# Cross attention biases of Q, K and V added by ScalarE, and the causal diagonal masked by a minimum on VectorE behind the exponential

## The chip, the cores and the metric

The kernel runs on one core of a Trainium2 chip, in one launch. The metric is the device time in microseconds (us). The core has TensorE (PE) for matrix products, VectorE (DVE), ScalarE (ACT), GpSimd (POOL), and SyncE (SP), which here only issues DMAs. Each engine executes its own instructions in order; engines wait for each other by semaphores. Products accumulate in PSUM, in eight banks of 128 x 512 numbers; everything else lies in SBUF.

## What is computed

Eight sequences of 512 tokens with 512 features go through a gated cross attention and then a gated block of causal attention and a mixture of experts. Cut to what the change touches, with `y` the layer norm of `x` and `c` the context:

```python
# cross attention, 16 heads of 32
Q = (y @ Wq + bq).reshape(B, S, 16, 32)
K = (c @ Wk + bk).reshape(B, S, 16, 32)
V = (c @ Wv + bv).reshape(B, S, 16, 32)
scores = einsum('bqhd,bkhd->bhqk', Q, K) / sqrt(32) + rel_bias[:, rel_pos]
attn = softmax(where(key_padding_mask, -inf, scores))
x = x + tanh(g_xattn) * (einsum('bhqk,bkhd->bqhd', attn, V).reshape(B, S, D) @ Wo + bo)
...
# causal attention inside the second block, 16 heads
att = einsum('bhqd,bhkd->bhqk', q, k) / sqrt(64)
att = softmax(where(tril(ones((t, t))), att, -inf))
out = einsum('bhqk,bhkd->bhqd', att, v)
```

## The kernel before

The kernel runs three passes one after the other: pass A is the cross attention (about 0 to 923 us of the span), pass B the causal attention (to about 1848 us), pass C the experts. The change touches A and B, which are built alike.

Both work on one sequence (a batch) after another. A batch has 64 units: 16 heads in four groups of four (HG), times four blocks of 128 keys (NT), head fastest, so a group of heads is 16 steps. Everything is written as steps: each engine's function `body` counts 64 steps, and in each it issues its part, so the order of instructions on an engine is that of the program. In step s, TensorE computes the scores of unit s-6 transposed (keys in partitions, queries in columns; L747 in A, L1504 to L1506 in B) into one of two banks `st_bank`, and, for the unit s of the next group, the scores again with the queries in partitions (L760, L1521 and L1522), from which VectorE takes the row maximum (L615, L1384; semaphore `lowered`), which is later folded into the transposed scores as one more row of the contraction. ScalarE takes the exponential of the transposed scores into `pt` or `probs` (L497, L1258; semaphore `exped`). GpSimd adds the probabilities of the four key blocks for the softmax's sum (L404, L407, L1169; `pooled`). Every four steps TensorE multiplies four heads' probabilities with V (L774, L1535, "the AV products"; `summed`).

Between these, TensorE's `fill` issues pieces of jobs that a planner has given to steps: the projections Q, K, V and the output projection O, transposes, and the spreading of the softmax sums. A job's result lies in one of three banks until it is evicted. Numbers of high precision are carried as two float16 parts: a high half, written by ScalarE (L464 and L471 in A, L1224 in B), and a low half, written by VectorE as value minus high half (L579, L1335). A product then takes three matmuls per 128 of the contraction (L693; L1425 to L1427).

In pass A the biases are added by TensorE: at the end of each of the jobs Q, K, V and O, one matmul L695 over 512 columns multiplies the two float16 halves of the bias with a tile of ones. With 16 such jobs in a batch and 8 batches these are 128. The end of a group of heads is evicted on a fixed schedule: ScalarE copies the AV result to `o_un` (L523), VectorE transposes and inverts the sums (L564 to L568), GpSimd multiplies `o_un` with them (L425, `normed`), ScalarE writes the high half `o_hi` (L528) and GpSimd the low half (L428), which the O products need.

In pass B a causal diagonal block has to hide the keys behind the query. For the transposed scores TensorE adds, in the first 128 columns of each unit, the product of `far` (the identity times 1e15) and `hidden` (-1e30 times 1e-15 where the key is hidden, else 0), one matmul L1505 of 128 columns for each of the 512 units; the exponential of the result is zero. For the row maxima VectorE adds `tri`. Since the blocks lie in the lower triangle, a unit of key block j has 512 - 128 j columns of queries.

A bank of scores is used again by the unit after the next one, so L747 and L1504 wait for the exponential of the unit before the last.

## Time and profile before

| | |
|---|---|
| time, median of 3 runs | 2419.53 us (2417.91 to 2424.08) |
| the profiled execution, its own time | 2419.89 us |
| its span | 2418.0 us |
| TensorE busy | 2171.5 us (90%) |
| VectorE busy | 1514.7 us (63%) |
| GpSimd busy | 1365.2 us (56%) |
| ScalarE busy | 1197.2 us (50%) |
| TensorE clock granted, mean | 0.955 of full speed |

The profile is of one execution. The span lies within the program's time, which is 1.9 us longer. A busy share of the whole span is a mean over three passes with different limits, so the rows below are taken from stretches within a pass. In rows, tiles of pass A begin with `a_`, of pass B with `b_`, of pass C with `c_`. The duration of a matmul in a row is that of one that stands in a pipeline: the next one starts before it has ended, and what a matmul costs a busy TensorE is the distance between two starts.

### The profile page before, as it was taken

Reading aid. Unit: us, or ns where it says so; the run is one execution under the profiler, and the core shown is the slowest. Engines: PE = TensorE matmul, PEld = TensorE weight load, DVE = VectorE, ACT = ScalarE, POOL = GpSimd, SP = SyncE. Lnnn points to the kernel's source line nnn. Section 1 sums busy time; section 2 is a strip of 40 time slices with the busy share of each in tenths; the row PEclk is TensorE's granted clock in tenths of the full one; section 3 lists DMA queues with packets and bytes.
Section 4 is the critical chain, followed back from the end, with each engine's and each line's share of the span. In section 5 each row is a group of like instructions: output and inputs, shape, how many; then the busy total and the mean of one; then the engine's idle time right before and its main releaser. Section 6 shows DMA issues by size and latency. Waiting matters only on the chain. (4 is left out here: it accounts for less than half of the span.)

```text
span 2418.0 us, 50305 instructions
## 1 busy us (share of the span) xinstructions
PE 2171.5 (90%) x12864; PEld 982.9 (41%) x12865; DVE 1514.7 (63%) x4218; ACT 1197.2 (50%) x2316; POOL 1365.2 (56%) x1452
## 2 busy tenths in 40 slices
PE   3899999999999963899999999999985797899997
PEld 1333333333333311344444444444432343455554
DVE  3788888887888843556565565555533678344443
ACT  3355555554555442355545454454544574455554
POOL 3267677677677670264655564565561565455554
PEclk7999999999999986899999999999997899899999
DMA  5413323232232203543434353352414576666665
GB/s 173 147 57 107 97 86 110 70 110 87 96 106 75 80 9 129 146 118 117 147 94 135 101 154 117 101 156 88 134 50 136 86 178 132 106 114 114 111 109 91
DMA packets 221402, 264.60 MB, mean 109 GB/s; under 512 B 37400, under 2 KB 163468, under 8 KB 220852
## 3 DMA queue, kind: packets, MB, share of 16 engines
q1 hardware_dynamic: 197612, 212.79, 29.2%
q0 software_dynamic: 22976, 48.38, 11.6%
q8 instruction: 106, 1.74, 0.3%
q14 instruction: 172, 1.41, 0.2%
q10 hardware_dynamic: 536, 0.28, 0.0%
HBM read 162.12 MB, written 86.80 MB: 103 GB/s over the span
## 5 line engine op out<-in xcount | busy, mean ns | idle before, releaser
L497 ACT ACTIVATE a_pt<-a_bank 128x512 f32<-128x512 f32 x512 | 305.1, 597 | 356.2 <-DVE a_bank L604 343.5
L1384 DVE CUSTOM_DVE_ANT_0 b_bank<-b_bank,b_tri 128x256 f32<-128x256 f32 (+3 forms) x512 | 253.7, 497 | 322.7 <-PE b_bank L1522 320.3
L615 DVE CUSTOM_DVE_ANT_0 a_bank<-a_bank,a_strip 128x512 f32<-128x512 f32 x512 | 354.2, 693 | 7.3 <-PE a_bank L760 4.6
L1169 POOL TENSOR_TENSOR b_acc<-b_acc,b_pt 128x256 f32<-128x256 f32 (+2 forms) x384 | 271.7, 725 | 104.6 <-ACT b_pt L1258 88.0
L407 POOL TENSOR_TENSOR a_acc<-a_acc,a_pt 128x512 f32<-128x512 f32 x256 | 317.8, 1270 | 14.6 <-ACT a_pt L497 11.3
L604 DVE TENSOR_TENSOR a_bank<-a_bank,a_band 128x256 f32<-128x256 f32 (+1 forms) x512 | 205.6, 402 | 132.0 <-PE a_bank L747 130.2
L1258 ACT ACTIVATE b_pt<-b_bank 128x256 f32<-128x256 f32 (+2 forms) x384 | 143.4, 381 | 202.1 <-PE b_bank L1506 199.0
L747 PE MATMUL a_bank<-a_q_stack,a_k_stack 128*128 128x512 f16 x512 | 197.7, 388 | 14.6 <-ACT a_pt L497 10.2
L760 PE MATMUL a_bank<-a_k_stack,a_q_stack 97*128 97x512 f16 x512 | 196.3, 384 | 3.6 <-DVE a_low L615 3.5
L1850 POOL DMA_INDIRECT out_dram<-c_z,c_to_row x72 | 114.1, 1585 | 139.6 <-DMA out_dram<-c_z,c_to_row 106.5
L1504 PE MATMUL b_bank<-b_q_stack,b_k_stack 96*128 96x256 f16 (+3 forms) x512 | 155.5, 304 | 9.5 <-ACT b_pt L1258 6.4
L404 POOL TENSOR_TENSOR a_acc<-a_pt 128x512 f32<-128x512 f32 x128 | 160.0, 1271 | 4.3 <-ACT a_pt L497 4.3
L1521 PE MATMUL b_bank<-b_k_stack,b_q_stack 96*128 96x256 f16 (+3 forms) x512 | 154.6, 302 | 5.3 <-DMA b_q_stack<-qk_rows 3.0
L425 POOL TENSOR_TENSOR a_o_un<-a_o_un,a_den 128x512 f32<-128x512 f32 x32 | 40.8, 1276 | 202.7 <-DVE a_den L568 202.7
L1184 POOL TENSOR_TENSOR b_o_un<-b_o_un,b_den 128x512 f32<-128x512 f32 x32 | 40.7, 1273 | 201.5 <-DVE b_den L1352 195.6
L1506 PE MATMUL b_bank<-b_q_stack,b_k_stack 97*128 97x256 f16 (+3 forms) x512 | 153.3, 300 | 0.0
L1522 PE MATMUL b_bank<-b_k_stack,b_q_stack 96*128 96x256 f16 (+3 forms) x512 | 153.2, 300 | 0.0
L774 PE MATMUL a_bank<-a_pt,a_v 128*32 128x512 f32 x1024 | 138.1, 612 | 1.4 <-ACT a_pt L497 1.4
L747 PEld LDWEIGHTS a_bank<-a_q_stack,a_k_stack 128*128 128x128 f16 x512 | 49.4, 97 | 186.6 <-ACT a_pt L497 116.9
L1258 ACT ACTIVATE b_acc<-b_bank 128x512 f32<-128x512 f32 x128 | 76.5, 597 | 94.4 <-PE b_bank L1506 94.3
L1505 PE MATMUL b_bank<-b_hidden,b_far 128*128 128x128 bf16 x512 | 112.7, 220 | 0.0
L2230 DVE TENSOR_TENSOR c_xt_lo<-c_bank,c_xt_hi 128x512 f16<-128x512 f32 x72 | 49.8, 691 | 99.8 <-ACT c_xt_hi L1969 98.6
(346 smaller groups left out, 5501.8 us busy)
## 6 DMA issues: line engine op xcount, KB each, us to landing
b_q_stack<-qk_rows SPq DMA_DIRECT2D x192, 128.0 KB, 2.7
a_q_stack<-qk_rows SPq DMA_DIRECT2D x96, 128.0 KB
a_k_stack<-qk_rows SPq DMA_DIRECT2D x96, 128.0 KB
b_k_stack<-qk_rows SPq DMA_DIRECT2D x96, 128.0 KB, 2.6
a_sums<-in_x SPq DMA_DIRECT2D x34, 256.0 KB, 3.2
qk_rows<-a_qk_hi SPq DMA_DIRECT2D x64, 128.0 KB, 1.7
qk_rows<-a_qk_lo SPq DMA_DIRECT2D x64, 128.0 KB, 1.8
out_dram<-a_sums SPq DMA_DIRECT2D x32, 256.0 KB, 2.0
```

Source lines behind the costliest of these rows:

```text
L404: nc.gpsimd.tensor_tensor(acc[:, hh, :], pt[:, (n - HG) % SLOTS, :], mine, ALU.add).then_inc(pooled, 1)
L407: nc.gpsimd.tensor_tensor(acc[:, hh, :], acc[:, hh, :], mine, ALU.add).then_inc(pooled, 1)
L497: nc.scalar.activation(pt[:, n % SLOTS, :], st_bank[n % 2][:], ACT.Exp).then_inc(exped, 1)
L604: nc.vector.tensor_tensor(st_bank[n % 2][:, c0:c1], st_bank[n % 2][:, c0:c1], band[:, h, at:at + c1 - c0], ALU.add).then_inc(biased, 1)
L615: nc.vector.tensor_tensor_reduce(out=max_bank[step % 2][:], in0=max_bank[step % 2][:], in1=strip[:, g * HG + hh, at:at + S], scale=-1.0, s ...
L747: mm(st_bank[n % 2][:], k_stack[:, h, j * P:(j + 1) * P], q_stack[:, h, :], start=True, stop=True).then_inc(scored, 1)
L760: mm(max_bank[step % 2][:], q_stack[0:MASK + 1, h, i * P:(i + 1) * P], k_stack[0:MASK + 1, h, :], start=True, stop=True).then_inc(maxed, 1)
L1169: nc.gpsimd.tensor_tensor(sums_of, sums_of, probs(n), ALU.add).then_inc(pooled, 1)
L1258: nc.scalar.activation(probs(n), st_bank[n % 2][:, 0:w], ACT.Exp).then_inc(exped, 1)
L1384: nc.vector.tensor_tensor_reduce(out=max_bank[step % 2][:, 0:w], in0=max_bank[step % 2][:, 0:w], in1=tri[:, at:at + w], scale=-1.0, scalar ...
L1504: mm(o, k_stack[0][0:LOW, h, j * P:(j + 1) * P], q_stack[0][0:LOW, h, j * P:], start=True, stop=False)
L1521: mm(o, q_stack[0][0:LOW, h, c], k_stack[0][0:LOW, h, 0:w], start=True, stop=False)
```

## The change

In pass A the matmul L695 is issued for the job O alone. The high half of Q and K is written in two steps: ScalarE's Identity reads the bank, scales, adds a bias that differs by partition, and writes a float32 row `qk_row` in SBUF; a Copy then writes the float16 high half from that row. VectorE's low half is `qk_row` minus the high half, from two tiles in SBUF, where it read the bank before. The bank of Q and K is free after ScalarE's Identity (`left_act`). The bias of V is added where the AV result is divided by its sum: the weights of a softmax row sum to one, so ScalarE adds the bias to `o_un` in place before it writes `o_hi`. The bias columns come by one DMA, and the setup of the row biases shrinks to that of O.

In pass B the matmul L1505 and its setup are gone. VectorE takes, between the exponential and all that reads it, the minimum of the unit's first 128 columns with a tile `seen`, which is 0 where the key is hidden and 3e38 elsewhere. GpSimd's sums and the AV products wait for this minimum (`masked`) and no longer for `exped`. It is issued at the start of step n+7 for unit n, ahead of the maximum of that step.

```diff
@@ pass A, ScalarE
-                    nc.scalar.activation(qk_hi[:, 2 * (n % 2) + part, :], src, ACT.Copy, scale=(q_scale if m == Q else 1.0 / WS)
-                                         ).then_inc(hi_done, 1)
+                    if kind == "first" and n == 0:
+                        act.wait_ge(b_scaled, 1)
+                    if n == G3:
+                        act.wait_ge(left_dve, before(kind, b, by_dve))
+                    elif n or kind != "first":
+                        act.wait_ge(left_dve, upto(kind, b, (m, (n - 1) % NG), by_dve))
+                    nc.scalar.activation(qk_row[:, part, :], src, ACT.Identity, scale=(q_scale if m == Q else 1.0 / WS),
+                                         bias=b_col[:, part, n:n + 1]).then_inc(left_act, 1)
+                    act.wait_ge(left_act, upto(kind, b, job, by_act))
+                    nc.scalar.activation(qk_hi[:, 2 * (n % 2) + part, :], qk_row[:, part, :], ACT.Copy).then_inc(hi_done, 1)
...
+                            nc.scalar.activation(o_un[:], o_un[:], ACT.Identity, bias=b_col[:, 2, g:g + 1]).then_inc(v_biased, 1)
+                            act.wait_ge(v_biased, groups + 1)
                             nc.scalar.activation(o_hi[:, g, :], o_un[:], ACT.Copy).then_inc(o_hi_done, 1)
@@ pass A, VectorE
-                    hi, lo, scale = qk_hi[:, slot, :], qk_lo[:, slot, :], (q_scale if m == Q else 1.0 / WS)
+                    nc.vector.tensor_tensor(qk_lo[:, slot, :], qk_row[:, int(m == K), :], qk_hi[:, slot, :], ALU.subtract
+                                            ).then_inc(left_dve, 1)
+                    return
@@ pass A, TensorE
-                    mm(o, lhs, rhs, start=(k == 0 and i == 0), stop=False)
+                    last = mm(o, lhs, rhs, start=(k == 0 and i == 0), stop=(k == NK - 1 and i == 2 and m != O))
                 if k == NK - 1:
-                    mm(o, *both, start=False, stop=True).then_inc(job_done, 1)
+                    if m == O:
+                        last = mm(o, ones[:], bias[:], start=False, stop=True)
+                    last.then_inc(job_done, 1)
@@ pass B, GpSimd
-                        pool.wait_ge(exped, b * UNITS + n + 1)
+                        pool.wait_ge(masked, b * UNITS + n + 1)
@@ pass B, VectorE
+                    n = step - L - 1
+                    if has_unit(kind, n):
+                        dve.wait_ge(exped, b * UNITS + n + 1)
+                        nc.vector.tensor_tensor(probs(n)[:, 0:P], probs(n)[:, 0:P], seen[:], ALU.min).then_inc(masked, 1)
                     if has_max(kind, step):
@@ pass B, TensorE
-                        mm(o[:, 0:P], far[:], hidden[:], start=False, stop=False)
...
-                        pe.wait_ge(exped, b * UNITS + n + 1)
+                        pe.wait_ge(masked, b * UNITS + n + 1)
```

ScalarE in the steady loop of pass A, from the Q eviction of a group (waits `a_kept0`) over that of K to the high half of the output. Before:

```order
L471 ACTIVATE a_qk_hi<-a_bank 128x512 [waits a_kept0,a_job_done]
L497 ACTIVATE a_pt<-a_bank 128x512 [waits a_pooled,a_biased]
L523 ACTIVATE a_o_un<-a_bank 128x512 [waits a_o_lo_done,a_summed]
L497 ACTIVATE a_pt<-a_bank 128x512 [waits a_pooled,a_biased]
L497 ACTIVATE a_pt<-a_bank 128x512 [waits a_pooled,a_summed,a_biased]
L497 ACTIVATE a_pt<-a_bank 128x512 [waits a_pooled,a_biased]
L471 ACTIVATE a_qk_hi<-a_bank 128x512 [waits a_kept1,a_job_done]
L497 ACTIVATE a_pt<-a_bank 128x512 [waits a_pooled,a_biased]
L528 ACTIVATE a_o_hi<-a_o_un 128x512 [waits a_normed]
```

After:

```order
L480 ACTIVATE a_qk_row<-a_bank,a_b_col 128x512 [waits a_left_dve,a_kept0,a_job_done]
L483 ACTIVATE a_qk_hi<-a_qk_row 128x512 [waits a_left_act]
L508 ACTIVATE a_pt<-a_bank 128x512 [waits a_pooled,a_biased]
L534 ACTIVATE a_o_un<-a_bank 128x512 [waits a_o_lo_done,a_summed]
L508 ACTIVATE a_pt<-a_bank 128x512 [waits a_pooled,a_biased]
L508 ACTIVATE a_pt<-a_bank 128x512 [waits a_pooled,a_summed,a_biased]
L508 ACTIVATE a_pt<-a_bank 128x512 [waits a_pooled,a_biased]
L480 ACTIVATE a_qk_row<-a_bank,a_b_col 128x512 [waits a_left_dve,a_kept1,a_job_done]
L483 ACTIVATE a_qk_hi<-a_qk_row 128x512 [waits a_left_act]
L508 ACTIVATE a_pt<-a_bank 128x512 [waits a_pooled,a_biased]
L539 ACTIVATE a_o_un<-a_o_un,a_b_col 128x512 [waits a_normed]
L541 ACTIVATE a_o_hi<-a_o_un 128x512 [waits a_v_biased]
```

Each eviction of Q or K is now two rows, the first with a wait for VectorE's last low half of the same kind, and the high half of the output has the bias ahead of it. The exponentials between them stand in the same order. (L480 and L483 are the two steps of Q and K, L508 the exponential, L534, L539 and L541 the work on `o_un`.)

VectorE in pass B, where the rotated part of a Q projection is evicted (`b_rc`, `b_qu_lo`). Before:

```order
L1382 REGISTER_ALU
L1384 ISA b_bank,b_low<-b_bank,b_tri 128x384 [waits b_maxed]
L1384 ISA b_low 128x1
L1316 REGISTER_ALU
L1323 TENSOR_TENSOR b_rc<-b_bank,b_rot 128x512 [waits b_rot_lo,b_hi_done]
L1335 SCALAR_TENSOR_TENSOR b_qu_lo<-b_bank,b_qu_hi 128x512
L1382 REGISTER_ALU
L1384 ISA b_bank,b_low<-b_bank,b_tri 128x256 [waits b_maxed]
L1384 ISA b_low 128x1
```

After:

```order
L1394 TENSOR_TENSOR b_acc<-b_acc,b_seen 128x128 [waits b_exped]
L1400 REGISTER_ALU
L1402 ISA b_bank,b_low<-b_bank,b_tri 128x384 [waits b_maxed]
L1402 ISA b_low 128x1
L1330 REGISTER_ALU
L1337 TENSOR_TENSOR b_rc<-b_bank,b_rot 128x512 [waits b_rot_lo,b_hi_done]
L1349 SCALAR_TENSOR_TENSOR b_qu_lo<-b_bank,b_qu_hi 128x512
L1394 TENSOR_TENSOR b_acc<-b_acc,b_seen 128x128 [waits b_exped]
L1400 REGISTER_ALU
L1402 ISA b_bank,b_low<-b_bank,b_tri 128x256 [waits b_maxed]
L1402 ISA b_low 128x1
```

Ahead of every maximum (L1384 before, L1402 after; one instruction and the read of its result) stands the minimum on `b_acc` or `b_pt` with its wait for the exponential, so a maximum is behind the exponential of an older unit.

TensorE in pass B, two steps' scores and maxima. Before:

```order
L1504 MATMUL b_bank<-b_q_stack,b_k_stack 128x512 [waits b_exped]
L1505 MATMUL b_bank<-b_hidden,b_far 128x128
L1506 MATMUL b_bank<-b_q_stack,b_k_stack 128x512
L1518 REGISTER_ALU
L1521 MATMUL b_bank<-b_k_stack,b_q_stack 128x256 [waits b_lowered]
L1522 MATMUL b_bank<-b_k_stack,b_q_stack 128x256
L1504 MATMUL b_bank<-b_q_stack,b_k_stack 128x384 [waits b_exped]
L1505 MATMUL b_bank<-b_hidden,b_far 128x128
L1506 MATMUL b_bank<-b_q_stack,b_k_stack 128x384
```

After:

```order
L1522 MATMUL b_bank<-b_q_stack,b_k_stack 128x512 [waits b_exped]
L1523 MATMUL b_bank<-b_q_stack,b_k_stack 128x512
L1535 REGISTER_ALU
L1538 MATMUL b_bank<-b_k_stack,b_q_stack 128x256 [waits b_lowered]
L1539 MATMUL b_bank<-b_k_stack,b_q_stack 128x256
L1522 MATMUL b_bank<-b_q_stack,b_k_stack 128x384 [waits b_exped]
L1523 MATMUL b_bank<-b_q_stack,b_k_stack 128x384
```

The matmul of `b_hidden` and `b_far` is gone from every unit; nothing else moved.

## Rows read from the trace of the kernel before

**Rows 1.** Busy us of PE, PEld, DVE, ACT, POOL in stretches; then granted clock and DMA.

```profile
200.00:800.00 600.00, 592.40 (x3190) 228.62 (x3188) 503.58 (x1359) 331.08 (x587) 427.01 (x396) 0.99 0.29 93
534.88:543.50 8.62, 8.62 (x48) 3.46 (x50) 8.55 (x24) 4.39 (x9) 6.80 (x6) 1.00 0.09 36
1340.40:1443.67 103.27, 101.27 (x704) 49.54 (x703) 61.56 (x179) 51.85 (x110) 58.55 (x77) 1.00 0.42 124
1786.00:1812.00 26.00, 19.65 (x177) 8.78 (x174) 5.90 (x20) 16.39 (x38) 20.06 (x26) 1.00 0.01 2
```

**Rows 2.** Timeline of TensorE in pass B: start, duration, operation.

```profile
1402.04 0.38 PE L1504 MATMUL b_bank<-b_q_stack,b_k_stack 96*128 96x512 f16 x1
1402.26 0.22 PE L1505 MATMUL b_bank<-b_hidden,b_far 128*128 128x128 bf16 x1
1402.32 0.38 PE L1506 MATMUL b_bank<-b_q_stack,b_k_stack 97*128 97x512 f16 x1
```

**Rows 3.** Groups by form, TensorE: line, operation, count, busy us, mean ns.

```profile
L1505 PE MATMUL b_bank<-b_hidden,b_far 128*128 128x128 bf16 x512 | 112.7, 220 | 0.0
```

**Rows 4.** Groups by form, ScalarE.

```profile
L1964 ACT ACTIVATE c_z<-c_z,c_entry 128x512 f32<-128x512 f32 x72 | 51.8, 719 | 16.7 <-DMA c_z<-z_all,c_from_row 16.7
...
L1995 ACT ACTIVATE c_z<-c_bank,c_entry 128x512 f32<-128x512 f32 x72 | 49.5, 687 | 79.8 <-DVE c_to_row L2240 49.8 <-PE c_bank L2403 30.0
...
L471 ACT ACTIVATE a_qk_hi<-a_bank 128x512 f16<-128x512 f32 x64 | 37.9, 593 | 24.1 <-PE a_bank L695 22.7
...
L528 ACT ACTIVATE a_o_hi<-a_o_un 128x512 f16<-128x512 f32 x32 | 19.9, 622 | 8.5 <-POOL a_o_un L425 8.5
```

**Rows 5.** Groups by form, VectorE.

```profile
L579 DVE SCALAR_TENSOR_TENSOR a_qk_lo<-a_bank,a_qk_hi 128x512 f16<-128x512 f32 x64 | 43.9, 686 | 25.0 <-ACT a_qk_hi L471 25.0
...
L1384 DVE CUSTOM_DVE_ANT_0 b_bank<-b_bank,b_tri 128x128 f32<-128x128 f32 x128 | 38.3, 299 | 75.2 <-PE b_bank L1522 74.0
```

**Rows 6.** Groups by form, GpSimd in pass B.

```profile
L1169 POOL TENSOR_TENSOR b_acc<-b_acc,b_pt 128x384 f32<-128x384 f32 x128 | 125.8, 996 | 16.0 <-PE b_bank L1535 15.7
...
L1169 POOL TENSOR_TENSOR b_acc<-b_acc,b_pt 128x256 f32<-128x256 f32 x128 | 90.0, 724 | 14.6 <-ACT b_pt L1258 14.0
...
L1169 POOL TENSOR_TENSOR b_acc<-b_acc,b_pt 128x128 f32<-128x128 f32 x128 | 56.8, 454 | 74.0 <-ACT b_pt L1258 74.0
...
L1184 POOL TENSOR_TENSOR b_o_un<-b_o_un,b_den 128x512 f32<-128x512 f32 x32 | 40.7, 1273 | 201.5 <-DVE b_den L1352 195.6 <-PE b_bank L1535 6.0
```

**Rows 7.** Timeline of VectorE in pass C.

```profile
1901.31 1.60 DVE L2049 TENSOR_TENSOR c_sel<-c_rest,c_logit 128x32 f32<-128x32 f32 x1
...
1925.21 2.14 DVE L2019 SCALAR_TENSOR_TENSOR c_d_lo<-c_d_stage,c_d_hi 128x1024 f16<-128x1024 f32 x1
```

**Rows 8.** Timeline of GpSimd in the same two places.

```profile
1900.70 0.97 POOL L1789 DMA_INDIRECT table<-c_record,c_place_i  x1 [0.30 <-issue]
1901.68 1.17 POOL L1770 TENSOR_TENSOR c_h_lo<-c_hid,c_h_hi 128x512 f16<-128x512 f32 x1
...
1925.08 1.17 POOL L1770 TENSOR_TENSOR c_h_lo<-c_hid,c_h_hi 128x512 f16<-128x512 f32 x1
```

**Rows 9.** Waits of TensorE over one batch of pass B (1340.40 to 1443.7).

```profile
PE b_bank L1425 <- DVE b_qu_lo L1335: 1.0, 1, 1.0
PE b_bank L1425 <- POOL b_o_lo L1187: 0.7, 1, 0.7
```

**Rows 10.** Waits of VectorE over the same batch.

```profile
DVE b_bank L1384 <- PE b_bank L1522: 40.5, 46, 2.1
```

**Rows 11.** Timeline of ScalarE in pass A, at step 15.

```profile
541.17 0.60 ACT L497 ACTIVATE a_pt<-a_bank 128x512 f32<-128x512 f32 x1 [0.48 <-DVE a_bank L604]
```

**Rows 12.** Timeline of TensorE at the same place.

```profile
541.82 0.39 PE L747 MATMUL a_bank<-a_q_stack,a_k_stack 128*128 128x512 f16 x1
```

**Rows 13.** Timeline of GpSimd in pass B, ahead of the last part of an output product.

```profile
1439.90 1.15 POOL L1187 TENSOR_TENSOR b_o_lo<-b_o_un,b_o_hi 128x512 f16<-128x512 f32 x1
```

More of the change, by code:

```diff
@@ L59, in unit_of, with pass_a @@
     return g, i, hh
-def pass_a(nc, x, ctxt, maskb, g_gate, wq, bq, wk, bk, wv, bv, wo, bo, strips, bands, far, side_rows, ident, x1, mask_rows,
+def pass_a(nc, x, ctxt, maskb, g_gate, wq, wk, wv, wo, b_cols, bo, strips, bands, far, side_rows, ident, x1, mask_rows,
            qk_rows):
@@ L79, in pass_a @@
         w_lo = sb("w_lo", [P, 4, NK, D], F16)
-        bias = sb("bias", [P, 4, D], F16)
+        bias = sb("bias", [P, D], F16)
+        b_col = sb("b_col", [P, 3, NG])
+        qk_row = sb("qk_row", [P, 2, S])
         ones = sb("ones", [P, P], F16)
@@ L192, in pass_a @@
         split_kinds = (CT, XT, Q, K)
-        on_act = (V, M)
+        on_act = (V, M, Q, K)
         ROUNDS = B - 2
@@ L216, in by_dve @@
         def by_dve(j):
-            return j[0] not in on_act
+            return j[0] not in (V, M)
         def ended(kind, step):
@@ L678, in product @@
                     pairs = ((w_hi[:, w, k, c], h[:, k, :]), (w_hi[:, w, k, c], l[:, k, :]), (w_lo[:, w, k, c], h[:, k, :]))
-                    both = (bias[:, w, c], ones[:].unsqueeze(1).broadcast_to([P, NT, P]))
                     if k == 0 and n < G3:
@@ L685, in product @@
                     pairs = ((h[:, k, c], w_hi[:, w, k, :]), (h[:, k, c], w_lo[:, w, k, :]), (l[:, k, c], w_hi[:, w, k, :]))
-                    both = (ones[:], bias[:, w, :])
                     if m == O:
@@ L810, in pass_b @@
         tri = sb("tri", [P, STRIP])
-        far = sb("far", [P, P], BF16)
-        hidden = sb("hidden", [P, P], BF16)
+        seen = sb("seen", [P, P])
         LOW = 3 * DH
@@ L854, in pass_b @@
                                                             sem("padded"))
[L855 to L856 removed]
+        norm_loaded, norm_scaled, sides_stored, masked = (sem("norm_loaded"), sem("norm_scaled"), sem("sides_stored"),
+                                                          sem("masked"))
         x_loaded, stats_done, mv_done, small_done, h_ready = (sem("x_loaded"), sem("stats_done"), sem("mv_done"),
@@ L1075, in body @@
                     weights(1)
-                    for dst, src in ((idn[:], ident), (swp[:], swap), (rot[:], cos_sin), (tri[:], causal), (den[:, 0:P], later)):
+                    for dst, src in ((idn[:], ident), (swp[:], swap), (rot[:], cos_sin), (tri[:], causal), (seen[:], later)):
                         sp.dma_start(dst, src).then_inc(const_loaded, 16)
@@ L1301, in _ @@
             act.wait_ge(norm_scaled, 1)
-            act.wait_ge(const_loaded, 80)
-            nc.scalar.activation(far[:], idn[:], ACT.Copy, scale=1e15).then_inc(far_set, 1)
-            nc.scalar.activation(hidden[:], den[:, 0:P], ACT.Copy, scale=1e-15).then_inc(far_set, 1)
             over(act, body)
@@ L2447 @@
     for name in ("x", "ctx_1024", "mask_BxS2_bf0", "g_xattn", "g_ffn") + tuple(
-            "L0_xattn_" + n for n in ("Wq", "bq", "Wk", "bk", "Wv", "bv", "Wo", "bo")):
+            "L0_xattn_" + n for n in ("Wq", "Wk", "Wv", "Wo", "bo")):
         give(name, inputs[name])
+    give("bias_columns", _np.stack([_np.asarray(inputs["L0_xattn_" + n]).reshape(NG, P).T for n in ("bq", "bk", "bv")], 1))
     rel = _np.asarray(inputs["L0_xattn_rel_bias"])
@@ L2496 @@
     give("causal", _np.where(_np.arange(STRIP)[None, :] - (NT - 1) * P <= _np.arange(P)[:, None], 0, -1e30).astype(_np.float32))
-    give("later", _np.where(_np.arange(P)[:, None] > _np.arange(P)[None, :], -1e30, 0).astype(_np.float32))
+    give("later", _np.where(_np.arange(P)[:, None] > _np.arange(P)[None, :], 0, 3e38).astype(_np.float32))
     out = nc.dram_tensor("out_0_dram", (B, S, D), F32, kind="ExternalOutput").ap()
@@ L2504 @@
     used = pass_a(nc, ap["x"], ap["ctx_1024"], ap["mask_BxS2_bf0"], ap["g_xattn"],
-           *[ap["L0_xattn_" + n] for n in ("Wq", "bq", "Wk", "bk", "Wv", "bv", "Wo", "bo")],
+           *[ap["L0_xattn_" + n] for n in ("Wq", "Wk", "Wv", "Wo")], ap["bias_columns"], ap["L0_xattn_bo"],
            ap["strips"], ap["bands"], ap["beyond"], ap["side_rows"], ap["ident"], out, mask_rows, qk_rows[0])
```

19 lines of the change are left out of this document (10 added, 9 removed).

## The prediction

> **What bounds the kernel now.** I read the busy times of stretches first, because the share over the whole span mixes three passes. In pass A TensorE is busy 592.4 of 600 us and VectorE 503.6 of them (84%), with the full clock granted [rows 1]. In one batch of pass B, from one 512-wide maximum at 1340.40 us to the same one of the next batch at 1443.67, it is 101.3 of 103.27 us, and VectorE 61.6 (60%), GpSimd 58.6 (57%) [rows 1]. So both passes go at TensorE's pace, and columns taken from it are worth time until another engine is late. The waits of TensorE in that batch are few: 1.0 us for a low half of VectorE, 0.7 us for GpSimd's low half of the output [rows 9]. VectorE waits for nothing long but TensorE's score products, 40.5 us [rows 10]; that is its whole reserve. Then I looked for places where the other engines have none: in pass A VectorE is busy 8.55 of 8.62 us behind the end of a group [rows 1].
>
> **What TensorE saves.** A matmul costs the distance to the next start. The 512-column L1504 starts at 1402.04 and its follower at 1402.26, so 0.22 us; L1505 starts there and L1506 at 1402.32, so 0.06 us [rows 2]. The 220 ns in the groups is the length in the pipeline and not the cost [rows 3]. Pass A loses 12 matmuls of 512 columns in each of 8 batches: 96 x 0.22 = 21.1 us, 2.6 a batch. Pass B loses 512 [rows 3]: 512 x 0.06 = 30.7 us, 3.8 a batch. The ceiling of the gain is 51.8 us.
>
> **What pass A adds.** ScalarE: a Q or K eviction was one operation of 0.593 us; an Identity with a bias column from PSUM takes 0.687, a copy to float16 from SBUF 0.622, so 0.72 more, 64 times, 46 us. The V bias is an Identity in place in SBUF, 0.719 us, 32 times, 23 us [rows 4]. ScalarE goes from 331 of 600 us [rows 1] by 69/8 = 8.6 a batch to about 63%; the sum is not on the path, but its place is. At step 15 the exponential starts at 541.17 and ends at 541.77, and TensorE's next score product starts at 541.82 [rows 11, 12]: there TensorE is just behind ScalarE, and an eviction or the V bias ahead of it delays TensorE. I count 0.35 us for two such places in a batch, half of the 0.72, since ScalarE idled 0.48 us before that exponential: 0.7. VectorE: the low half takes 0.686 us now [rows 5] and reads two SBUF tiles then, for about the same time alone. But it can collide with GpSimd (below), which is busy 427 of 600 us [rows 1], with sums longer than those of rows 6; eight a batch, mostly with slack in front of the maximum: 0.5. In the stretch where VectorE has no idle [rows 1] the matmuls saved in three jobs, 3 x 0.22 = 0.65, buy nothing. Back: 1.85 of 2.6, so -0.8 a batch, -6.3 in eight. Ends: -21 if everything hides; +10 if each of the 12 longer ScalarE places cost 0.3 (12 x 0.3 x 8 = 29, less 21, rounded up). Start and end of the pass I take at nothing; the bias activations at the start stand beside the weight loads.
>
> **What pass B adds.** 512 minima on VectorE. The nearest row is the maximum over the same 128x128, 0.299 us [rows 5]; I take 0.29, 18.6 us a batch. It is not that alone. The minimum reads two SBUF tiles, and the trace shows what such an operation does beside GpSimd: L2049, 128x32, takes 1.60 us at 1901.31, ending at 1902.91, while GpSimd's L1789 ends at 1901.67 and L1770 runs to 1902.85; L2019 at 1925.21 takes 2.14 us, and L1770 had begun at 1925.08 for 1.17 [rows 7, 8]. So VectorE stood until GpSimd was through, in the first case through two operations back to back. In pass B GpSimd is busy 58.55 of 103.27 us with sums of 1.00, 0.72 and 0.45 us, 16 of each in a batch, and 16 longer ones of up to 1.27 [rows 1, 6]. A minimum that comes at a random moment waits the sum of the squares halved over the period: (16 x (0.99 + 0.52 + 0.21) + 16 x 1.6) / 2 / 103.27 = 0.26 us; I take 0.25, 16 us a batch. Ends: 0 (GpSimd waits for `masked`, so the sum of a unit begins when its minimum is through and could be over before the next) and a whole sum, 0.7 (always behind one).
>
> VectorE is then without idle for 103.27 - 40.5 = 62.8 us now, plus 18.6, plus 16: 97.4, of a batch that TensorE could do in 103.27 - 3.8 = 99.5. The minimum fits, and hardly. Behind it on VectorE stands the maximum, whose `lowered` TensorE awaits two steps later; ahead of GpSimd's sum and the AV product it adds its own length.
>
> The Trainium skill ("SBUF — State Buffer", Who interferes with whom) calls this an exclusive lock on a pair of ports that VectorE needs for two SBUF inputs and GpSimd always, and says that issue order decides who blocks. The trace agrees with it at both places of rows 7 and 8; by the rule alone, without the durations, neither 0 nor 0.7 can be preferred.
>
> What comes back in a batch of B: GpSimd's chain ahead of the last part of an output product, where L1187 runs from 1439.90 to 1441.05 and TensorE waits 0.7 us for it [rows 9, 13]: four operations, each later by a minimum, 4 x 0.3 = 1.2. The last steps of a batch, where minima, low halves and rotations stand close on VectorE: I estimate four steps late by a minimum, 1.25. ScalarE's evictions of V, which TensorE waits for anyway: 0.35. That is 2.8 of 3.8: -1.0 a batch, -8.3 in eight (eight times 0.06 x 64 - 2.8). In the last body GpSimd is the bound, 20.1 of 26 us busy [rows 1]; its sums there run back to back, and each gets a minimum of 0.29 us in front: 16 x 0.29 = +4.6. Pass B: -3.7. Pass C has the same instructions: 0.
>
> **Sum.** 2419.9 (the profiled execution, 0.4 above the median of 2419.5) - 6.3 - 3.7 = 2409.9; I say 2410.
>
> **The rivals.** I: everything hides. VectorE's 40.5 us of reserve speak for it, and that a unit's sum follows its own minimum, so that collisions are rare; the full VectorE of rows 1 speaks against it in A, the last body in B. Then 2419.9 - 51.8 = 2368; with A as I have it and the last body too, 2419.9 - 6.3 - 30.7 + 4.6 = 2388.
>
> II (slower): the port makes VectorE the bound of pass B. A minimum finds GpSimd in an operation, and a next one is issued before VectorE gets its turn, as at 1901.68 [rows 8]. The point from which it decides is the mean wait at which VectorE is full: (99.5 - 62.8 - 18.6) / 64 = 0.28 us, hardly above my 0.25. At 0.4 us VectorE needs 62.8 + 18.6 + 25.6 = 107.0 us a batch, 3.7 more than now: +30 us, with the last body's +5 and A's -6: 2449. At 0.7, 126 us a batch, it would be 2600, but GpSimd's sums wait for `masked` themselves and can't run ahead that far. For it speaks that VectorE at 98% can't be had without losses in an in-order queue; against it that TensorE is two steps ahead of the maximum.
>
> III: pass A returns its gain and a little more because ScalarE's two-step evictions delay exponentials (+10 for A, B as forecast): 2419.9 + 10 - 4 = 2426.
>
> IV: the gain of A is whole, with B as forecast: 2419.9 - 21.1 - 3.7 = 2395.
>
> **Chances and range.** A difference under 0.3%, 7.3 us, can't be told from none here. Forecast (2400 to 2420): 0.40. Rival I: 0.10. II: 0.27. III: 0.10. IV: 0.13. Faster holds I, IV and somewhat over half of the forecast: 0.45. Within 0.3%: the rest of the forecast and a little of III: 0.21. Slower: II and most of III, 0.34. The range reaches from between both cases of I to the price of II: 2380 to 2450; the likeliest case's own range is 2400 to 2420.
>
> **What would show it.** Right in A: a steady batch is shorter by about 0.8 us, ScalarE's share rises to about 63%, and no low half of Q or K is much over 0.7 us but some. Right in B: minima of 0.29 us where GpSimd is idle and up to 1.5 us where it is not, with a mean of 0.5 to 0.6; a batch of 102.2 us; VectorE over 85% busy; the last steps of the pass longer. If the mean of the minima is 0.3, rival I is right; if it is 0.7 or more and TensorE waits for L1402, rival II. The forecast is wrong in its main step if pass B's batch is over 104 or under 100 us.

## The result and the profile after

The changed kernel takes 2459.0 us (median of 4 runs, 2452.01 to 2464.66) where the kernel before takes 2419.8 (4 runs, 2417.91 to 2424.08): a ratio of 1.0155, 95% interval 1.0129 to 1.0181. It is slower by 39 us, outside the stated range of 2380 to 2450. The forecast was 2410. One run of the kernel with pass B's change alone was slow (2897 us, at a mean clock of 0.736 where its others had 0.94) and is left out below.

The span grew from 2418.0 to 2457.8 us. To see where, I read one event that occurs once in 16 steps of both passes, VectorE's transpose of the softmax sums (L564 and L1348 before, L577 and L1362 after), and took the distances between its starts in the two timelines:

```
stretch                                         before    after
start of the span to the first one of pass A    126.8     130.7    +3.9
first to last of pass A                         776.7     782.8    +6.1
last of A to first of B                         141.7     145.0    +3.3
first to last of pass B                         770.1     793.7   +23.7
rest (pass C)                                   602.7     605.6    +2.8
```

So most of it is in pass B, some in pass A, and pass C and the starts, in which nothing was added for the batches, hold a few us. Such stretches also vary between the kernels: pass C has the same instructions in all of those below and took 602.7 to 610.8 us. The view of busy times answers to [rows 1]; columns are those there. The first row is a stretch of pass A, the second and third are two batches of pass B, the fourth its last body:

```profile
200.00:800.00 600.00, 577.78 (x3088) 219.39 (x3085) 510.97 (x1342) 373.19 (x651) 436.12 (x392) 0.99 0.29 92
...
1163.17:1268.79 105.62, 100.16 (x640) 46.16 (x639) 86.48 (x246) 52.12 (x110) 60.21 (x76) 0.98 0.41 121
1268.79:1379.33 110.54, 101.43 (x640) 46.55 (x639) 85.67 (x246) 52.03 (x110) 60.30 (x76) 0.97 0.39 116
...
1800.23:1852.21 51.98, 40.00 (x265) 13.87 (x264) 40.53 (x102) 23.86 (x56) 33.62 (x42) 0.85 0.08 26
```

TensorE has 64 instructions fewer in a batch of B (640 for 704) and a longer batch: 105.6 and 110.5 us for 103.3 and 106.8. VectorE's busy time went from 61.6 to 86.5 us a batch, 24.9 more. In A, ScalarE went from 331 to 373 of 600 us, and TensorE from 592 to 578. The groups by form, VectorE and ScalarE of the kernel after:

```profile
L1394 DVE TENSOR_TENSOR b_pt<-b_pt,b_seen 128x128 f32<-128x128 f32 x384 | 231.6, 605 | 29.7 <-ACT b_pt L1275 19.0 <-issue 10.3
...
L591 DVE TENSOR_TENSOR a_qk_lo<-a_qk_row,a_qk_hi 128x512 f16<-128x512 f32 x64 | 64.9, 1013 | 31.6 <-ACT a_qk_hi L483 31.5
...
L480 ACT ACTIVATE a_qk_row<-a_bank,a_b_col 128x512 f32<-128x512 f32 x64 | 43.7, 684 | 22.5 <-PE a_bank L707 22.5
...
L483 ACT ACTIVATE a_qk_hi<-a_qk_row 128x512 f16<-128x512 f32 x64 | 40.4, 632 | 2.0
L1394 DVE TENSOR_TENSOR b_acc<-b_acc,b_seen 128x128 f32<-128x128 f32 x128 | 40.0, 312 | 2.7 <-ACT b_acc L1275 2.7
...
L539 ACT ACTIVATE a_o_un<-a_o_un,a_b_col 128x512 f32<-128x512 f32 x32 | 22.9, 715 | 5.6 <-POOL a_o_un L428 5.6
```

The minimum is 0.605 us in the mean on `b_pt` and 0.312 on `b_acc`, 0.53 over all 512. The low half of Q and K grew from 0.686 [rows 5] to 1.013. In the timeline a single minimum can be followed. VectorE of the kernel after, in pass B:

```profile
1462.91 1.23 DVE L1394 TENSOR_TENSOR b_pt<-b_pt,b_seen 128x128 f32<-128x128 f32 x1 [0.45 <-ACT b_pt L1275]
1464.06 0.28 DVE L1402 CUSTOM_DVE_ANT_0 b_bank<-b_bank,b_tri 128x128 f32<-128x128 f32 x1
```

and GpSimd in the same place:

```profile
1461.82 1.06 POOL L1186 TENSOR_TENSOR b_acc<-b_acc,b_pt 128x384 f32<-128x384 f32 x1
1462.84 1.15 POOL L1204 TENSOR_TENSOR b_o_lo<-b_o_un,b_o_hi 128x512 f16<-128x512 f32 x1
```

The minimum was issued at 1462.91, just behind the start of L1204, and ended at 1464.14, 0.15 us behind that operation's end at 1463.99: it stood for nearly its whole length. The maximum behind it began only then, at 1464.06. So it is with the other long minima. Of the 203 above 0.40 us that have a row of their own in the timeline, 196 ended 0.14 to 0.16 us behind the end of a GpSimd operation; the other seven ended within rows that put several GpSimd operations together. The 188 that had no GpSimd operation beside them took 0.27 to 0.29 us. What TensorE waits for in a batch of B (1379.33 to 1483.32), to be held against [rows 9]; columns: total us, times, longest:

```profile
PE b_bank L1443 <- POOL b_o_lo L1204: 1.2, 1, 1.2
PE b_bank L1552 <- DVE b_pt L1394: 1.1, 2, 0.7
PE b_bank L1443 <- DVE b_qu_lo L1349: 1.0, 1, 1.0
PE b_bank L1538 <- DVE b_low L1402: 0.7, 1, 0.7
```

and what VectorE waits for in it, against [rows 10]:

```profile
DVE b_bank L1402 <- PE b_bank L1539: 14.2, 21, 1.6
```

TensorE waits in many small places, for the minimum itself (in front of the AV products L1552), for the maximum behind it, and for GpSimd. VectorE waits 14 us for TensorE's score products in this batch, where it waited 40 before, so it is not full.

### The profile page after: what moved, and what is told of

It is laid out like the page before. It is cut to its first block and busy times, and to the rows that moved or that the text cites. A ratio compares the mean times of both kernels' runs of the same rounds, so it can differ in the third digit from the quotient of the medians.

```text
span 2457.8 us, 49917 instructions
## 1 busy us (share of the span) xinstructions
PE 2159.5 (88%) x12256; PEld 944.8 (38%) x12257; DVE 1737.3 (71%) x4731; ACT 1258.9 (51%) x2410; POOL 1399.5 (57%) x1452
## 5 line engine op out<-in xcount | busy, mean ns | idle before, releaser
L508 ACT ACTIVATE a_pt<-a_bank 128x512 f32<-128x512 f32 x512 | 304.3, 596 | 314.8 <-DVE a_bank L619 306.1
L1186 POOL TENSOR_TENSOR b_acc<-b_acc,b_pt 128x256 f32<-128x256 f32 (+2 forms) x384 | 280.8, 738 | 169.4 <-DVE b_pt L1394 155.8
L1402 DVE CUSTOM_DVE_ANT_0 b_bank<-b_bank,b_tri 128x256 f32<-128x256 f32 (+3 forms) x512 | 252.8, 494 | 129.6 <-PE b_bank L1539 127.7
L410 POOL TENSOR_TENSOR a_acc<-a_acc,a_pt 128x512 f32<-128x512 f32 x256 | 327.4, 1306 | 13.5 <-ACT a_pt L508 9.7
L1394 DVE TENSOR_TENSOR b_pt<-b_pt,b_seen 128x128 f32<-128x128 f32 x384 | 231.6, 605 | 29.7 <-ACT b_pt L1275 19.0
L765 PE MATMUL a_bank<-a_q_stack,a_k_stack 128*128 128x512 f16 x512 | 199.6, 392 | 28.8 <-ACT a_pt L508 22.0
L407 POOL TENSOR_TENSOR a_acc<-a_pt 128x512 f32<-128x512 f32 x128 | 166.4, 1318 | 5.0 <-ACT a_pt L508 5.0
L765 PEld LDWEIGHTS a_bank<-a_q_stack,a_k_stack 128*128 128x128 f16 x512 | 49.5, 97 | 219.0 <-ACT a_pt L508 166.6
```

Of the source, the lines that this page charges most:

```text
L407: nc.gpsimd.tensor_tensor(acc[:, hh, :], pt[:, (n - HG) % SLOTS, :], mine, ALU.add).then_inc(pooled, 1)
L410: nc.gpsimd.tensor_tensor(acc[:, hh, :], acc[:, hh, :], mine, ALU.add).then_inc(pooled, 1)
L508: nc.scalar.activation(pt[:, n % SLOTS, :], st_bank[n % 2][:], ACT.Exp).then_inc(exped, 1)
L765: mm(st_bank[n % 2][:], k_stack[:, h, j * P:(j + 1) * P], q_stack[:, h, :], start=True, stop=True).then_inc(scored, 1)
L1186: nc.gpsimd.tensor_tensor(sums_of, sums_of, probs(n), ALU.add).then_inc(pooled, 1)
L1394: nc.vector.tensor_tensor(probs(n)[:, 0:P], probs(n)[:, 0:P], seen[:], ALU.min).then_inc(masked, 1)
```

## The experiments

Each kernel ran beside the kernel before on the same chip. All ratios are to that kernel, with 95% intervals. A "steady batch" is one in the middle of a pass in which no loop turns, from VectorE's first transpose of the sums in it to the same one of the next. The first four kernels separate the passes and take the minimum apart.

**Pass A alone.** All edits of pass A of the change, pass B as before.

> Only the change of pass A; pass B as in the kernel before. By the two traces the stretch up to the last transpose of pass A (903.47 us before, 913.50 after) costs 10 us, with a steady batch about 1 us longer. Theory P (the shared port is the price in both passes: two SBUF inputs on VectorE beside GpSimd): about 2430, with the low halves of Q and K at a mean of 1.0 us. Rival R (pass A is harmless by itself, its delay in the trace comes from the load of weights at the start): 2417 to 2423.

Measured: 2435.05 us (4 runs), ratio 1.0063 (1.0045 to 1.0080). It is slower by 16 us, 5 above theory P's figure, so pass A is not harmless. Of the 16.7 us between the two profiled executions the start takes 2.9 (126.8 to 129.7 us to the first transpose) and the rest of pass A 5.7; the other 8 lie in the passes B and C, which are unchanged. The steady batch of A went from 101.2 to 102.1. The low halves are 1.018 us in the mean.

**Pass B alone.** All edits of pass B, pass A as before.

> Only the change of pass B; pass A as in the kernel before. By the two traces pass B (from the last transpose of A to the last of B) costs 27 us, 7 of them in its last body. If the two parts add up, 2446 to 2450, with the minimum at a mean of about 0.53 us. If they do not add up (a pass that starts at another phase is slower), clearly less, under 2440.

Measured: 2449.61 us (3 runs, 2444.87 to 2454.76), ratio 1.0125 (1.0093 to 1.0157), slower by 30 us; minima 0.53 us in the mean. 16 and 30 exceed the 39 of both together a little; the intervals allow for it.

**Neither matmul nor minimum in pass B.**

```diff
-                        mm(o[:, 0:P], far[:], hidden[:], start=False, stop=False)
```

No minimum is put in; sums and AV products wait for `exped`, as before.

> Pass B without the matmul of far and hidden and without the minimum: the hidden keys of the diagonal blocks are left in the sums and products. Everything else as in the kernel before. It shows what TensorE's saved columns are worth where nothing replaces them. Full worth 30.7 us: 2389. If most of the saved time is covered by waits for the other engines anyway, 2405 or more.

Measured: 2399.68 us (4 runs), ratio 0.9916 (0.9899 to 0.9932), 20 us faster, between the two expectations. The steady batch of B falls from 103.3 to 100.4 us, 2.9 of the 3.8 that I counted. So about a quarter of TensorE's saving in a steady batch, and a third over the kernel (20 of 30.7 us), does not come back even where nothing is added.

**The minimum replaced by an operation with one input.**

```diff
-                        nc.vector.tensor_tensor(probs(n)[:, 0:P], probs(n)[:, 0:P], seen[:], ALU.min).then_inc(masked, 1)
+                        nc.vector.transpose(probs(n)[:, 0:P], probs(n)[:, 0:P]).then_inc(masked, 1)
```

> The change of pass B alone, with the minimum replaced by a transpose in place of the same 128x128 tile, which reads one SBUF tile and waits at the same place and releases the same readers; the diagonal is not masked. Theory P (the wait for the port is what costs): near 0.28 us each at the least and at the most, and the time falls from that of the minimum by some 20 us or more, to 2400 to 2425. Rival V (VectorE's own time and the longer chain exponential, minimum, sum, AV product cost it, the port is a side effect): within 8 us of the kernel with the minimum, 2438 to 2450.

Measured: 2408.02 us (4 runs), ratio 0.9948 (0.9929 to 0.9968). The two forms of the stand-in, from the groups by form:

```profile
L1376 DVE STREAM_TRANSPOSE b_pt<-b_pt 128x128 f32<-128x128 f32 x384 | 117.1, 306 | 45.6 <-ACT b_pt L1257 37.8 <-issue 6.4
...
L1376 DVE STREAM_TRANSPOSE b_acc<-b_acc 128x128 f32<-128x128 f32 x128 | 37.8, 296 | 2.6 <-ACT b_acc L1257 2.6
```

It is in the same place in the order, waits for and releases the same, has about the length that the minimum has alone (0.27 to 0.31 us at all 512 places), and 42 us of the change are gone (2408 against 2450). What is left over the kernel with nothing in its place is 8 us. It is also issued beside GpSimd's operations as the minimum is: 251 of the stand-ins came while one had 0.3 us or more to run, and they took 0.30 or 0.31 us. That is theory P, for pass B: the price is the wait of an operation with two inputs in SBUF for GpSimd, called the port from here on. That wait is only 0.53 - 0.30 = 0.23 us in the mean. Two batches beside each other, VectorE's busy time the third number of a row; first the minimum (pass B alone, 1150.07 on), then the stand-in (1142.68 on):

```profile
1150.07:1254.07 104.00, 98.53 (x640) 45.57 (x639) 86.92 (x244) 51.91 (x110) 60.40 (x76) 1.00 0.41 123
```

```profile
1142.68:1243.65 100.97, 97.95 (x640) 45.72 (x639) 73.84 (x244) 51.80 (x110) 58.84 (x76) 1.00 0.43 126
```

What TensorE's matmuls wait for in these two batches, the longer waits; first with the minimum:

```profile
PE b_bank L1425 <- POOL b_o_lo L1186: 1.2, 1, 1.2
PE b_bank L1534 <- DVE b_pt L1376: 1.1, 2, 0.7
PE b_bank L1520 <- DVE b_low L1384: 0.7, 1, 0.7
PE b_bank L1534 <- DVE b_acc L1376: 0.4, 1, 0.4
PE b_bank L1469 <- DVE b_low L1384: 0.3, 1, 0.3
```

```profile
PE b_bank L1425 <- POOL b_o_lo L1186: 0.8, 1, 0.8
PE b_bank L1534 <- DVE b_acc L1376: 0.6, 2, 0.4
```

All else in the two lists is alike (1.0 us for `b_qu_lo`, 0.4 for an exponential). So 0.9 us more stand in front of the AV products L1534, 1.0 behind the maximum (`b_low`), and 0.4 in front of the output product L1425.

**Neither matmuls nor additions in pass A.** L695 is issued for O alone; the three biases are left out.

> Pass A without the 96 bias matmuls of Q, K and V and with nothing in their place: these three biases are left out, the evictions are those of the kernel before. Pass B and C as before. The columns are worth 21.1 us at most. If pass A is TensorE's alone, 2399; if VectorE's full stretches give it back, as pass B gave back 11 of 30.7 us, 2405 to 2415.

Measured: 2409.74 us (8 runs), ratio 0.9953 (0.9938 to 0.9969). The time fell by 10 us, within the second expectation, but the steady batches show another thing: 98.7 us for 101.2, 2.5 of the 2.6 that I counted. From the first transpose of A to its last the saving is 16 us; the start took 3.0 us more in this run, and the unchanged pass B 4.8. Where runs differ by several us in stretches with the same instructions, the distance of the steady batches is the better measure, and I use it below.

**The low half from the bank again.**

```diff
-                    nc.vector.tensor_tensor(qk_lo[:, slot, :], qk_row[:, int(m == K), :], qk_hi[:, slot, :], ALU.subtract
-                                            ).then_inc(left_dve, 1)
-                    return
+                    hi, lo, scale = qk_hi[:, slot, :], qk_lo[:, slot, :], (q_scale if m == Q else 1.0 / WS)
```

Two more things come with this edit and are not in the cut: the bank of Q and K is free only after VectorE's low half, and ScalarE no longer waits for VectorE before it writes `qk_row`. In the kernel with pass A's whole change that wait cost ScalarE no time: the Identity waited only for TensorE.

> The change of pass A alone (2435 with it), but the low half of Q and K is again the bank minus the high half: one input from PSUM, one from SBUF; the bias is missing in the low half, so hi plus lo has none. ScalarE's two-step evictions and the V bias stay. Theory P (the wait for GpSimd's port inside the low half, 0.33 us in the mean, is what pass A pays): under 2420. Rival S (ScalarE's additions, 0.72 us an eviction and 0.72 us a V bias, delay the exponentials): 2428 or more.

Measured: 2431.97 us (6 runs), ratio 1.0049 (1.0032 to 1.0065): 3 us under pass A's whole change. The steady batch is 101.2 us against 102.1. Rival S holds: in pass A the port is about 0.9 us a batch, and the larger part is elsewhere.

**The V bias alone on ScalarE.** Q and K keep their matmuls.

> The kernel before with the bias of V alone moved to ScalarE (32 matmuls of 512 columns less, 7.0 us at most; 32 in-place additions of 0.72 us on ScalarE more); Q and K keep their bias matmuls. If the V part is harmless: 2413 to 2418. If the addition in front of the high half of the output delays GpSimd's low half and the output product behind it: 2420 to 2428.

Measured: 2426.63 us (10 runs), ratio 1.0023 (1.0008 to 1.0039). It is slower although 32 matmuls are gone. In the profiled execution (2430.11 us, near the top of the ten) the start took 134.3 us to the first transpose, 7 more than before, which is most of the difference; its steady batch is 101.3 us, where 98.7 plus two thirds of 2.5 would be 100.4. So four additions cost 0.9 us a batch.

**Two-step evictions without the V bias.** The change of A with the addition on `o_un` left out.

> The change of pass A alone with the addition of the V bias left out: two-step evictions of Q and K and the low half from two SBUF tiles stay. The whole change of A costs 25 us over the kernel with neither matmuls nor additions (2435 against 2410). By the steady batches of the runs so far (98.7 us with neither, 101.2 with the low half from the bank, 102.1 with all) the port has 0.9 us a batch. If the V bias has another 0.9 (V alone: 101.26 where 100.4 were due), the steady batch is here 101.2 and the time 2426 to 2430. If the two-step evictions are harmless, it is 99.6 and 2415.

Measured: 2436.35 us (4 runs), ratio 1.0052 (1.0034 to 1.0070). The steady batch is 101.2 us as expected. The time is above the expected 2430: in the profiled execution pass C, which has nothing changed, took 610.8 us for 602.7, pass B 3.8 more than before, and the start 2.2.

The steady batches of pass A put together, from these five kernels (a sum in which each part is taken to add to the others; the evictions' part is what is left and was not run alone):

```
nothing in place of the 12 matmuls             98.7
eight two-step evictions                       +1.6  (the rest)
four additions of the V bias                   +0.9  (102.1 - 101.2; with Q and K on matmuls 101.3 - 100.4)
the low half waiting for GpSimd                +0.9  (102.1 - 101.2)
all of it                                     102.1
before                                        101.2
```

Where this lands is seen in what TensorE's matmuls wait for in the batch of pass A alone (231.51 to 333.60); those of the kernel before and of the one without additions have no wait for ScalarE in theirs:

```profile
PE a_bank L765 <- ACT a_pt L508: 1.3, 4, 0.5
PE a_bank L685 <- DVE a_xt_lo L594: 0.6, 1, 0.6
```

TensorE's score products L765 wait for ScalarE's exponential four times. The weight loads in front of them show more of the same wait (18.6 us in 24 places; 12.3 in 16 in the kernel before), which is not all TensorE's time.

**The mask added to the score bank.**

```diff
-                        mm(o[:, 0:P], far[:], hidden[:], start=False, stop=False)
...
+                    n = step - L
+                    if has_unit(kind, n):
+                        dve.wait_ge(scored, b * UNITS + n + 1)
+                        o = st_bank[n % 2][:, 0:P]
+                        nc.vector.tensor_tensor(o, o, seen[:], ALU.add).then_inc(masked, 1)
...
-                        act.wait_ge(scored, b * UNITS + n + 1)
+                        act.wait_ge(masked, b * UNITS + n + 1)
```

> Pass B with the diagonal masked by VectorE ahead of the exponential: it adds a tile of 0 and -1e30 to the first 128 columns of the score bank, so one input is PSUM and one SBUF; the matmul of far and hidden is gone, sums and AV products wait for the exponential as before. Pass A as before. Theory P says that this form never waits for GpSimd: about 0.30 us each without a tail; the sum is then near that of the one-input stand-in, 2408, or a few us more because the exponential is now behind VectorE: 2405 to 2415, faster than the kernel before. If the exponential's delay holds TensorE's next score products: 2420 to 2440.

Measured: 2410.49 us (6 runs), ratio 0.9955 (0.9937 to 0.9974): faster than the kernel before. From its groups by form:

```profile
L1377 DVE TENSOR_TENSOR b_bank<-b_bank,b_seen 128x128 f32<-128x128 f32 x512 | 152.2, 298 | 159.9 <-PE b_bank L1506 156.9
```

It is as much work on VectorE, 512 operations over 128x128 with a tile of SBUF as the second input; the first is in PSUM, and it takes 0.27 to 0.33 us at every place. The steady batch of B is 101.6 us. Its last body is longer, 48.1 us against 44.9. There the exponential is behind it, and the granted clock was 0.85 against 0.98; which of the two weighs more was not taken apart.

**The minimum behind the maximum.**

```diff
-                    n = step - L - 1
-                    if has_unit(kind, n):
-                        dve.wait_ge(exped, b * UNITS + n + 1)
-                        nc.vector.tensor_tensor(probs(n)[:, 0:P], probs(n)[:, 0:P], seen[:], ALU.min).then_inc(masked, 1)
                     if has_max(kind, step):
...
+                    n = step - L - 1
+                    if has_unit(kind, n):
+                        dve.wait_ge(exped, b * UNITS + n + 1)
+                        nc.vector.tensor_tensor(probs(n)[:, 0:P], probs(n)[:, 0:P], seen[:], ALU.min).then_inc(masked, 1)
                     for job in ended(kind, step - 1):
                         evict(kind, b, job)
```

> The change of pass B alone, with the minimum of a step issued behind the maximum of that step and ahead of the low halves, instead of ahead of both. If it is the wait for GpSimd in front of the maximum that holds TensorE, the time falls clearly below that of the change of B alone (2450), to 2425 to 2440. If VectorE's total is the bound, or the sums behind the minimum, it stays at 2446 to 2456.

Measured: 2484.68 us (4 runs), ratio 1.0254 (1.0238 to 1.0269). Both expectations missed it by 30 us. The view of one line shows who waited for the minimum, in total us and times:

```profile
  POOL b_acc L1168: 196.4, 253
  PEld b_bank L1534: 66.9, 64
  PE b_bank L1534: 60.1, 60
```

In the kernel with the early minimum TensorE's AV products L1534 waited 16.4 us in 28 places. So the chain exponential, minimum, AV product is short of time as well, and the place at the front of the step was the better one.

**The stand-in at the late place.** The same transpose as above, behind the maximum.

> The one-input stand-in (a transpose in place, no mask) at the late place, behind the maximum of the step. Early it ran at 2408, and the minimum at 2450; late the minimum ran at 2485. If the port alone is the price at either place, this is within 8 us of the early stand-in, 2404 to 2416, and the minimum waits longer for GpSimd where it is late. If the place itself costs (the sums and AV products behind it come later), it is well above, 2425 to 2445.

Measured: 2431.01 us (10 runs), ratio 1.0033 (1.0017 to 1.0049). The place costs 23 us without any wait for the port (2431 against 2408), and the port another 54 at that place (2485 against 2431), although the late minimum is no longer in the mean: (189.5 + 70.3) / 512 = 0.51 us each, for 0.53. So the mean wait does not set the price. That it is set by what stands behind each one is likely, but was not followed place by place.

**A version meant to beat both.** Pass B with the mask added to the bank, and the K bias dropped: it adds the same number to all scores of a query, and the softmax cancels it.

```diff
+                    last = mm(o, lhs, rhs, start=(k == 0 and i == 0), stop=(k == NK - 1 and i == 2 and m == K))
                 if k == NK - 1:
-                    mm(o, *both, start=False, stop=True).then_inc(job_done, 1)
+                    if m != K:
+                        last = mm(o, *both, start=False, stop=True)
+                    last.then_inc(job_done, 1)
```

> A version meant to beat both: pass B as with the mask added to the score bank by VectorE ahead of the exponential (2410), and in pass A the bias of K dropped together with its 32 matmuls: it adds to all scores of a query the same number, which the softmax cancels; the biases of Q, V and O stay matmuls. 32 matmuls at the 2.5 us a batch that 12 of them were worth give 0.8 us a batch, 6 to 7 us: 2402 to 2406.

Measured: 2402.98 us (5 runs, 2400.98 to 2407.49), ratio 0.9920 (0.9907 to 0.9934). It beats the kernel before by 0.8% and the changed one by 2.3%. Its steady batch of pass A is 100.3 us, 0.9 less, and that of B 101.6.

## Why the prediction was wrong

The forecast was -6 us for pass A and -4 for pass B. Alone they measured +16 and +30.

**What bounds the kernel, and what the matmuls are worth.** Right in pass A's steady batches: 2.5 of 2.6 us came back when nothing was added (over the pass 16 of 21). The 0.65 us that I gave up for the stretch in which VectorE is always busy was not lost. In pass B the worth is 2.9 of 3.8 us; the sum had it whole.

**ScalarE's additions in pass A: "for two such places in a batch ... 0.7".** This term was mis-sized: it measured 2.5 us a batch (1.6 for the evictions, 0.9 for the V bias), about 0.2 for each of twelve places. I had looked at one place with ScalarE just in front of TensorE [rows 11, 12] and counted two of twelve. With the port's 0.9, where I had 0.5, pass A gives back 3.4 us a batch of 2.5, and I had 1.85 of 2.6. The forecast for A was -6; alone it measured +16, of which 0.9 x 8 = 7 are in the batches and 3 in the start, and the rest lies in stretches in which the runs vary.

**The minimum.** Its own length was right (0.29; the least in the trace is 0.25 to 0.27), and the mean wait for the port too: I took 0.25 us, measured 0.23. That is in part luck, since the working had all minima alike: the 384 on `b_pt` took 0.605 us, a wait of some 0.3, and the 128 on `b_acc` 0.312, hardly any. VectorE's busy time grew by 24.9 us a batch where 34.6 was my sum of length and wait (18.6 + 16); part of the length lies under the neighbour's, as the minima and maxima overlap in the rows by some 0.08 us.

**"What comes back in a batch of B ... is 2.8 of 3.8."** This is the step that failed. By the same count 4.5 of 3.8 come back in the steady batch: 0.9 before anything is added, 0.6 for an operation of the minimum's length, 3.0 for the port (104.0 us measured, 102.2 forecast). With the wait's mean right, I let it act in three places and by hand-picked amounts, and took everything else as cover. The AV products and the maximum, where TensorE waits 1.9 us more with the minimum than with the stand-in, were named in none of them; the chain to the output product, for which I took 1.2, waits 0.4 more. The stand-in shows what the minimum costs without the port: about 0.6 us in a steady batch (101.0 against 100.4). The port adds 3.0 us to the steady batch (104.0 against 101.0), and more in others: the first batch of pass B alone took 106.1 us against 100.0, the last body 52.1 against 45.1, the two batches in which the loop turns 13 us more together. Over the pass it is 37 us in the profiled executions (796.4 against 759.7), over the kernel 42. A mean of 0.23 us hides waits of up to 1.1 (the longest minimum took 1.39), and TensorE is held at the AV products, at the maximum, and at the low half of the output.

**The last body: "each gets a minimum of 0.29 us in front: 16 x 0.29 = +4.6".** The size was near, +7.1, and the reason wrong. The stand-in is in front of the same sums and its last body takes 45.1 us, the same as before. It is the port there too, in part by way of the clock: granted were 0.85 with the minimum (pass B alone, 1788.22 to 1840.34) and 0.94 with the stand-in (1757.24 to 1802.36).

**Rival II** named the port and nearly the time (2449), but not the way in which it acts, and the nearness is luck: it had +35 for pass B from a mean wait of 0.4 us and a full VectorE, and -6 for pass A. Its condition was wrong: it was to decide only above a mean wait of 0.28 us, where VectorE would be full. The mean was 0.23, VectorE still waited 14 us in a batch for TensorE, and the kernel was slower all the same. That an engine's work fits into a batch does not show that its waits are harmless. Nor did GpSimd's next operation go ahead of a waiting minimum: the longest one, 1.39 us at 1733.76, ended 0.14 us behind the one operation it was issued beside (L1169, 1733.74 to 1735.01).

**What the prediction read in rows 7 and 8.** The Trainium skill ("SBUF — State Buffer", Who interferes with whom) says that a VectorE instruction with two inputs in SBUF contends with a GpSimd instruction that reads SBUF, and one with at most one input there does not. That holds here: the minimum of 1462.91 stood until GpSimd's operation was through, and the mask in PSUM and the one-input transpose never did. It also says that issue order decides who blocks, and the prediction found this at both places. At the first it is not so: L2049 was issued at 1901.31 and GpSimd's L1770 only at 1901.68, and L1770 went first. And L1789, a DMA issue beside which L2049 was already waiting, had not held the operation before, which has two inputs in SBUF too:

```profile
1901.03 0.18 DVE L2046 TENSOR_TENSOR c_ex<-c_logit,c_top 128x32 f32<-128x32 f32 x1
```

Why a waiting operation is passed there and not in pass B stays open.

**A part that no term had.** Twice in pass B, when the loop over pairs of batches turns, TensorE pauses. In the kernel with pass B's change alone it stood still from 1314.4 for 5.5 us with nothing in the profile that it waited for ("issue"). The first of a row's last three numbers is the granted clock:

```profile
1314.00:1318.00 4.00, 0.42 (x8) 0.00 (x0) 1.08 (x3) 1.55 (x5) 4.00 (x5) 0.78 0.70 253
1318.00:1322.00 4.00, 2.09 (x8) 1.08 (x9) 0.77 (x2) 0.38 (x1) 1.00 (x2) 0.50 0.24 76
1322.00:1326.00 4.00, 4.00 (x22) 1.95 (x20) 1.96 (x9) 1.25 (x3) 1.45 (x2) 0.86 0.36 103
```

The kernel before, at its turn, where TensorE waited 2.0 us for an exponential:

```profile
1310.00:1314.00 4.00, 3.25 (x14) 1.72 (x15) 0.76 (x2) 0.97 (x2) 2.38 (x3) 0.67 0.87 310
1314.00:1318.00 4.00, 4.00 (x29) 1.84 (x27) 1.76 (x5) 0.94 (x3) 2.78 (x5) 0.90 0.23 68
```

The granted clock falls within the pause and is at 0.50, which is 1.2 of 2.4 GHz, until about 3 us after TensorE goes on at 1319.9; the 512-column products then start 0.42 us apart instead of 0.22. The batches with a turn took 111.8 and 113.1 us there. In the ten kernels whose pass B is unchanged or that have the stand-in or the bank form, they took 103.7 to 109.7, so a part of this is variation; that VectorE's later queue makes the pause longer is possible but was not taken apart. In the last body of the changed kernel the clock is 0.85 in the mean against 0.98 before.

**What stays open.** Why the late minimum loses 54 us to the port with a mean wait like the early one's; how much of pass A's two-step evictions is the longer eviction and how much its place; the few us by which starts and unchanged passes differ between kernels; and what the longer code of VectorE has in the pauses at the loop's turn.

## What to carry to other kernels

Before moving work to VectorE where GpSimd is busy more than half of the time, look at where its inputs lie: with two in SBUF the operation queues behind GpSimd's, with one of them in PSUM it does not. Here a mask of as many operations was 30 us slower than the kernel before in the one form and 9 us faster in the other, and the one-input stand-in at the place of the slow form puts the difference down to the wait. A mean wait that fits into an engine's idle time says nothing of the critical path; run a stand-in of the same length and place without the suspected cost, and something with nothing in its place, and the two differences size the terms. And before a bias or mask is moved to another engine, ask if it is needed at all: the K bias cancels in the softmax.

## What the runs showed of the hardware

- A VectorE operation with both inputs in SBUF stood for GpSimd's operation to end, up to its whole length: 128x128 minima ran from 0.25 to 1.39 us and 128x512 low halves from 0.68 to 1.81 us. One 128x2048 low half of the weights (L555 of the changed kernel) took 5.8 us, where it took 2.6 in the kernel before: issued at 27.17, it was passed by three of GpSimd's casts, which began at 27.35, 28.33 and 29.53, one behind the other. A 128x128 transpose from SBUF to SBUF (0.27 to 0.31 us) and an addition with one input in PSUM (0.27 to 0.33 us) never did, at 512 places each.
- GpSimd's operations are hardly longer beside them: the 384-wide sums 1.016 us for 0.996, the 256-wide ones 0.742 for 0.724.
- In a pause of TensorE of 5.5 us the granted clock fell to 0.50, and it stayed there for about 3 us of work (1319.9 to 1323).
